# Dealing the weight preparation of a DLRM tower anew over the prologue and steps 0 to 6

## The reference, cut to what matters

```
e  = stack of 26 table rows per sample            # 512 x 26 x 64, gathered by ids
x  = layer_norm(dense @ Wd.T, gd, bd)             # 512 x 128
y  = layer_norm(e @ Ws.T, gs, bs)                 # 512 x 26 x 128
y  = layer_norm(y^T @ Wsi, gsi, bsi)^T            # 512 x 32 x 128
T  = concat(x, y)                                 # 33 vectors of 128 per sample
Z  = lower triangle of T T^T                      # 528 products per sample
z  = layer_norm(Z @ Wl.T, gl, bl)[:384]
h  = relu(concat(z, dense) @ W_top1 + b_top1)     # 512
h  = relu(h @ W_top2 + b_top2)                    # 256
out = h @ W_top3
```

## Time and profile before

| | us |
|---|---|
| median of 3 runs | 297.45 |
| lowest, highest | 296.03, 299.9 |
| span of the profiled execution, first to last instruction | 185.4 |
| the rest of the median, outside the span | 112.05 |
| PE / DVE / ACT / POOL busy | 148.0 / 130.1 / 106.9 / 104.3 |
| mean granted clock of TensorE | 0.936 |

### The profile page before, as it was taken

One profiled execution on the slowest core, in us unless ns is written; L12 is line 12 of the kernel. 1 busy time (PEld: TensorE's weight loads), 2 busy tenths in 40 slices (PEclk: granted clock), 3 DMA queues, 4 the chain that ended last, 5 costly groups with the idle time before them and its releaser, 6 DMA issues.

```text
span 185.4 us, 4668 instructions
## 1 busy us (share of the span) xinstructions
PE 148.0 (80%) x1825; PEld 113.2 (61%) x1825; DVE 130.1 (70%) x300; ACT 106.9 (58%) x245; POOL 104.3 (56%) x111
## 2 busy tenths in 40 slices
PE   0089877977969947459996978899799799977995
PEld 0084544434549544419794947569596666877994
DVE  6269659772959594908697999579799967943142
ACT  1202435594868486866667877585877857831230
POOL 3778777877878777777777777777840000020000
PEclk9999999996999669855999999999999999997899
DMA  5816334141111112311111123111111100110000
GB/s 153 294 33 194 137 58 161 32 139 26 34 21 29 24 28 61 61 27 27 28 33 23 32 58 64 28 28 25 28 25 40 33 7 11 27 38 0 0 0 0
DMA packets 6003, 9.59 MB, mean 52 GB/s; under 512 B 2303, under 2 KB 3538, under 8 KB 5854
## 3 DMA queue, kind: packets, MB, share of 16 engines
q0 software_dynamic: 3392, 3.45, 10.3%
q1 hardware_dynamic: 2232, 5.08, 9.1%
q10 hardware_dynamic: 358, 0.78, 1.1%
HBM read 8.01 MB, written 0.00 MB: 43 GB/s over the span
## 4 chain that ended last, share of the span: by engine, by line
PE 40%; ACT 23%; DVE 19%; issue 11%; DMA 5%; ACTq 1%; DVEq 0%
PE psB L318 11%; ACT Zs L639 10%; DVE B L831 4%; ACT U L600 4%; DMA dense_sb<-in_dense 4%; PE psG L284 4%; DVE qA L809 4%; DVE prod L802 3%; PE psZ L333 3%; PE psW L352 3%; PE psU L299 3%; DVE ssB L838 3%; ACT sdB L617 2%; PE psB L520 2%; PE psZ L424 2%
## 5 line engine op out<-in xcount | busy, mean ns | idle before, releaser
L257 POOL DMA_INDIRECT g_sb<-in_table,row_id x104 | 102.8, 989 | 31.7 <-issue 31.4
L831 DVE TENSOR_TENSOR B<-psB,bias 128x512 f32<-128x512 f32 x31 | 20.0, 686 | 26.2 <-PE psB L318 26.2
L639 ACT ACTIVATE Zs<-psZ 32x264 f32<-32x264 f32 x59 | 36.3, 616 | 2.1 <-PE psZ L333 1.0
L318 PE MATMUL psB<-U,ws_g 64*128 64x512 f32 x64 | 20.9, 735 | 15.3 <-ACT U L600 15.2
L611 ACT ACTIVATE sqB<-B 128x512 f32<-128x512 f32 x31 | 19.1, 632 | 23.1 <-DVE B L831 23.1
L299 PE MATMUL psU<-wsi_x,g_sb 128*128 128x192 f32 (+4 forms) x128 | 23.3, 330 | 7.3 <-DVE g_sb L824 7.3
L299 PEld LDWEIGHTS psU<-wsi_x,g_sb 128*128 128x128 f32 x128 | 20.9, 206 | 11.1 <-DVE g_sb L824 11.0
L284 PEld LDWEIGHTS psG<-gram,sT 128*128 128x128 f32 x104 | 14.0, 207 | 14.5 <-ACT sT L587 10.0
L850 DVE TENSOR_TENSOR T<-B,rB 128x512 f32<-128x512 f32 x31 | 21.5, 692 | 1.1
L838 DVE TENSOR_REDUCE ssB<-sqB 128x16 f32<-128x512 f32 x32 | 21.7, 677 | 0.1
L284 PE MATMUL psG<-gram,sT 128*128 128x128 f32 x104 | 17.2, 308 | 0.7 <-ACT sT L587 0.7
(11 more groups left out here) (159 smaller groups left out, 226.7 us busy)
## 6 DMA issues: line engine op xcount, KB each, us to landing
g_sb<-in_table,row_id POOLq DMA_INDIRECT x104, 2.5
wl_sb<-in_wl SPq DMA_DIRECT2D x1, 1280.0 KB, 6.0
w_sb<-in_w SPq DMA_DIRECT2D x2, 512.0 KB, 5.4
w_sb<-in_w SPq DMA_DIRECT2D x1, 768.0 KB, 4.5
small_sb<-in_small SPq DMA_DIRECT2D x1, 615.5 KB, 4.1
dense_sb<-in_dense ACTq DMA_DIRECT2D x1, 512.0 KB, 7.3
Zt<-Zs SPq DMA_DIRECT2D x3, 80.0 KB
Zt<-Zs SPq DMA_DIRECT2D x3, 70.0 KB
```

The source lines that it names most:

```text
L257: pool.indirect_dma_start(g_sb[:, k, h * DSP:(h + 1) * DSP], None, table, bass.IndirectOffsetOnAxis(row_id[:, 2 * k + h:2 * k + h + 1], 0) ...
L318: pe.matmul(psB[h][:, :], ws_g[h * DSP:(h + 1) * DSP, :], U[h * DSP:(h + 1) * DSP, u % 2, :], start=not (last and h == 0), stop=True).then ...
L639: act.activation(to, product, ACT.Copy).then_inc(Z_kept, 1)
L831: dve.tensor_tensor(B[:, h, :].rearrange("p (s j) -> p s j", j=PROJ), psB[h][:, :].rearrange("p (s j) -> p s j", j=PROJ), bias[:, :].rearr ...
```

## The change

It moves work and two orders; what is computed stays. The parts:

1. `am`, `dj` and `gg` are made by VectorE ahead of `wsi_c`, `ws_g` after nine `spread`s; the two gain and shift passes over `xn` come after `scale_a(0)`; `wl_off` is made at the end of the prologue, not in step 3.
2. `wl` is loaded when `dense` has landed, not after the 8th gather.
3. ScalarE sums the five `wl` pieces in the prologue (before: steps 1 and 2), scales them in steps 0, 1, 2 (before: 4 and 5), and takes the shift row in step 2 (before: 5).
4. `hd` is no longer made in the prologue and step 0 and biased in place in steps 5 to 8; it leaves PSUM with its bias in steps 4 (two), 5 and 6, from `dense_part` in steps 3 (two), 4 and 5. `linear(0)` and `variance(0)` now wait for it.
5. The x transposes go to psZ and stand in step 0 between `transposes(1)` and `project(0)`; `shift_part` moves to the prologue and step 0, `bias_part` to step 2, `b1_z` to step 3, `w1_g` from steps 4 to 6 to steps 2 to 4, the statistics of the shift row from step 3 to step 1.
6. `deviation_w` and `relu2` go behind `keep_u` and `rows_out`; `recip_w` goes to the end of its VectorE step.
7. In each step ScalarE's preparation stands behind `rows_out`, ahead of `squares_b`, not at the step's end.

```diff
@@ sync queue
-            sp.wait_ge(gathered[3], 32)
+            sp.wait_ge(d_dense, 16)
             sp.dma_start(wl_sb[:, :, :], wl).then_inc(d_wl, 16)
@@ TensorE
             def project(u):
...
-                    pe.wait_ge(xT_ready, 1)
+                    pe.wait_ge(x_stat, 4)
...
             def linear(b, lo, hi):
...
                         pe.wait_ge(m_kept, 1)
+                        pe.wait_ge(hd_ready, K1 - 1)
...
             def variance(b):
...
-                    pe.wait_ge(bz_ready, 1)
+                    pe.wait_ge(hd_ready, K1)
...
             def dense_part(f):
                 if f == 0:
                     pe.wait_ge(d_w1d, 16)
-                if f >= 2:
+                    pe.wait_ge(m_kept, 1)
+                elif f == 1:
+                    pe.wait_ge(bz_ready, 1)
+                else:
                     pe.wait_ge(hd_ready, f - 1)
...
-            dense_part(0)
-            dense_part(1)
...
             norms(0)
-            x_part()
-            dense_part(2)
+            shift_part(0, 2)
...
+                if t == 0:
+                    x_part()
                 project(t)
...
                 if t == 0:
-                    dense_part(3)
+                    shift_part(2, CW)
                 if t == 1:
                     x_sum()
-                    shift_part(0, 2)
                 if t == 2:
-                    shift_part(2, CW)
+                    bias_part()
                 if t == 3:
-                    bias_part()
+                    dense_part(0)
+                    dense_part(1)
+                if t == 4:
+                    dense_part(2)
+                if t == 5:
+                    dense_part(3)
@@ ScalarE
             def keep_hd(f):
                 act.wait_ge(hd_done, f + 1)
-                act.activation(hd[:, f, :], psD[f][:, :], ACT.Copy).then_inc(hd_ready, 1)
+                act.activation(hd[:, f, :], psD[f][:, :], ACT.Identity, bias=b1_z[:, f:f + 1]).then_inc(hd_ready, 1)
...
+            def prepare(t):
+                if t == 0:
+                    act.wait_ge(x_tr, 1)
+                    act.activation(xT[:, :], psZ[:, :], ACT.Copy).then_inc(xT_ready, 1)
+                    act.wait_ge(w_prep, 7)
+                    scale_wl(0)
+                    scale_wl(1)
+                if t == 1:
+                    scale_wl(2)
+                    scale_wl(3)
+                if t == 2:
+                    keep_x()
+                    scale_wl(4)
+                    keep_m()
+                if t == 4:
+                    act.wait_ge(bz_ready, 1)
+                    keep_hd(0)
+                    keep_hd(1)
+                if t == 5:
+                    keep_hd(2)
+                if t == 6:
+                    keep_hd(3)
...
             rows_out(0)
+            act.wait_ge(d_wl, 16)
+            for jj in range(CW - 1):
+                sum_wl(jj)
             deviation_a(0)
-            keep_hd(2)
+            sum_wl(CW - 1)
...
-                if late and j == 0 and b:
-                    relu2(b - 1)
-                if late and j == 2:
-                    deviation_w(b)
                 keep_u(t)
                 if t + 1 < UNITS:
                     rows_out(t + 1)
                 else:
                     third_squares(0)
+                if late and j == 0 and b:
+                    relu2(b - 1)
+                if late and j == 2:
+                    deviation_w(b)
+                prepare(t)
...
-                if 5 <= t < 5 + K1:
-                    f = t - 5
...
-                    act.activation(hd[:, f, :], hd[:, f, :], ACT.Identity, bias=b1_z[:, f:f + 1]).then_inc(hd_biased, 1)
@@ VectorE
-                if late and j == 2:
-                    recip_w(b)
...
-                if t == 3:
+                if t == 1:
                     dve.wait_ge(m_done, 1)
...
-                if t == 4:
+                if t == 3:
                     dve.wait_ge(bz_done, 1)
...
+                if late and j == 2:
+                    recip_w(b)
+                if 2 <= t < 2 + KZ:
+                    k = t - 2
```

More of the change, by code:

```diff
@@ L690, in keep_hd, with sum_wl, scale_wl @@
                 act.wait_ge(hd_done, f + 1)
[L691 to L694 removed]
+                act.activation(hd[:, f, :], psD[f][:, :], ACT.Identity, bias=b1_z[:, f:f + 1]).then_inc(hd_ready, 1)
+            def sum_wl(jj):
+                act.activation(wl_g[:, jj, :], wl_sb[:, jj, :], ACT.Identity,
+                               accum_out=wl_sum[:, jj:jj + 1]).then_inc(wl_summed, 1)
+            def scale_wl(jj):
+                act.activation(wl_g[:, jj, :], wl_sb[:, jj, :], ACT.Identity, bias=wl_off[:, jj:jj + 1],
+                               scale=gg[:, jj:jj + 1]).then_inc(wl_scaled, 1)
@@ new lines, in keep_x, with keep_m @@
+            def keep_x():
+                act.wait_ge(x1_done, 1)
+                act.wait_ge(fills, 5)
+                act.activation(Zt[EXTRA:EXTRA + 2, :, :, 0, :],
+                               psH[EXTRA:EXTRA + 2, :].rearrange("p (b h s) -> p b h s", b=BLOCKS, h=2),
+                               ACT.Identity, bias=one_row[EXTRA:EXTRA + 2, :]).then_inc(x1_ready, 1)
+            def keep_m():
+                act.wait_ge(m_shift, 1)
+                act.wait_ge(wl_scaled, CW)
+                act.activation(wl_g[0:NA, 0, :], psW[0:NA, :], ACT.Identity, bias=m_off[0:NA, :],
+                               scale=g_i[0:NA, :]).then_inc(m_kept, 1)
@@ L954, in _ @@
             dve.tensor_reduce(wsi_sum[:, :], wsi, AX, ALU.add).then_inc(w_prep, 1)
-            dve.wait_ge(d_rows, 16)
-            dve.wait_ge(w_prep, 3)
-            dve.tensor_tensor(ws_g[:, :], ws_c[:, :], gs_b, ALU.mult).then_inc(w_prep, 1)
+            one_j3 = one_j.rearrange("p (c j) -> p c j", c=CW)
+            dve.tensor_scalar(dj[:, :, :], one_j3, b_i, None, ALU.mult)
+            dve.tensor_scalar(am[:, :, PROJ], at_x, b_i, None, ALU.mult)
+            dve.tensor_scalar(am[:, :, PROJ + 1], b_j, b_i, float(E), ALU.mult, ALU.mult)
+            dve.tensor_scalar(gg[:, :], g_j, g_i, None, ALU.mult).then_inc(w_prep, 1)
+            dve.wait_ge(w_prep, 4)
+            for jj in range(CW):
+                last = dve.scalar_tensor_tensor(out=am[:, jj, 0:PROJ], in0=one_i, scalar=b_j[:, jj:jj + 1],
+                                                in1=dj[:, jj, :], op0=ALU.mult, op1=ALU.add)
+            last.then_inc(am_ready, 1)
             dve.scalar_tensor_tensor(
@@ L993, in _ @@
             last.then_inc(x_stat, 1)
+            dve.wait_ge(bias_done, 1)
+            dve.tensor_copy(bias[:, :], psU[:, 0:PROJ]).then_inc(bias_kept, 1)
+            mult_a(0)
+            sums_a(0)
+            recip_a(0)
+            scale_a(0)
             dve.wait_ge(x_stat, 4)
@@ L999, in _ @@
                               bd_b.rearrange("p (o e) -> p o e", o=1).broadcast_to([P, 4, E]), ALU.add).then_inc(x_col, 1)
-            dve.wait_ge(bias_done, 1)
-            dve.tensor_copy(bias[:, :], psU[:, 0:PROJ]).then_inc(bias_kept, 1)
-            mult_a(0)
-            sums_a(0)
-            recip_a(0)
-            scale_a(0)
-            one_j3 = one_j.rearrange("p (c j) -> p c j", c=CW)
-            dve.tensor_scalar(dj[:, :, :], one_j3, b_i, None, ALU.mult)
-            dve.tensor_scalar(am[:, :, PROJ], at_x, b_i, None, ALU.mult)
-            dve.tensor_scalar(am[:, :, PROJ + 1], b_j, b_i, float(E), ALU.mult, ALU.mult)
-            dve.tensor_scalar(gg[:, :], g_j, g_i, None, ALU.mult).then_inc(w_prep, 1)
-            dve.wait_ge(w_prep, 6)
-            for jj in range(CW):
-                last = dve.scalar_tensor_tensor(out=am[:, jj, 0:PROJ], in0=one_i, scalar=b_j[:, jj:jj + 1],
-                                                in1=dj[:, jj, :], op0=ALU.mult, op1=ALU.add)
-            last.then_inc(am_ready, 1)
+            dve.wait_ge(wl_summed, CW)
+            dve.scalar_tensor_tensor(out=wl_off[:, :], in0=wl_sum[:, :], scalar=-1.0 / FLIN, in1=gg[:, :],
+                                     op0=ALU.mult, op1=ALU.mult).then_inc(w_prep, 1)
             def step(t):
```

47 lines of the change are left out of this document (7 added, 40 removed).

## The result

| | us |
|---|---|
| before, median of its runs beside these | 298.67 |
| changed kernel, median of 4 runs | 287.25 (286.18 to 291.6) |
| ratio, with its 95% interval | 0.9617 [0.9528, 0.9706] |
| forecast | 290.65, range 289.0 to 295.2 |
| span of the changed kernel's profiled execution, and that execution's own time | 284.4, 286.18 |

The change makes the kernel 3.8% faster, by 11.4 us. The forecast had the direction, and 6.8 us. Some runs of every kernel are a few per cent slower than its others; the medians hold all runs, the ratios leave the slow ones out.

A forecast was written before the change was run, and what follows sets the result against it. A loop over TensorE, ScalarE and VectorE was taken to bound the kernel, with gathers as ceiling. 6.95 + 0.25 = 7.2 us, less 0.4 for the clock, is 6.8: span 178.6 plus 112.05 gives 290.65, range 289.0 to 295.2.

The forecast's parts named there:

- The ceiling: At units 4 to 12, gather landings limit the gain: unit 4 at most 2.4 us earlier, unit 12 at most 6.95.
- the forecast's own signs of being wrong: Wrong if unit 8 starts over 1 us behind its gather, half clock exceeds two steps behind 46, or gathers move.
- The 112 us around the span: Time outside the profiled span of 185.4 us, taken as the same 112.05 us before and after the change.
- Steps 3 to 6: Unit 4 to unit 8: 30.0 + 0.4 + 1.4 us from 48.6 gives 80.4, then 2.5 of wait for the gather.
- the evictions with bias: On ScalarE in its wait for add_b: each between 0.60 and 0.68 us; two in step 4 are free.
- Step 7: An in-place bias (0.68) and the root (0.37) leave ScalarE's list ahead of keep_u(8): with overlap 0.8 us saved.
- steps 8 to 14: recip_w on VectorE at keep_u(9) costs 0.66 us, relu at keep_u(10) saves 0.5, unit 12 to the end saves 0.25.
- Steps 0 to 2: TensorE is ready for unit 4 well before 48.6, then idles about 2.5 us until its gather lands.
- the price of a half clock: At project(7), behind a 2.5 us wait: between 0 and 1.5 us, less 0.6 of slack; 0.4 taken.
- A: Clock rival: new waits at units 4 and 8 put three steps at half clock, 3.35 us lost, 293.6; chance 0.22.
- C: Slower: gather waits in steps 3 to 14 drop the clock, 2.15 us a step, 313 with all twelve; chance 0.05.
- B: Waits change places in steps 3 to 6; only the 2.4 us up to unit 4 come through, 295.05; chance 0.14.

The follow-up runs named there:

- e1: The kernel before, unedited, run once more for its profile: 299.85 us, ratio 0.9987, span 297.4.
- e4: Changed kernel with only block 0 gathered by GpSimd (26 of 104 gathers), other blocks' rows read by plain loads: 192.69 us.
- e5: Kernel before with only block 0 gathered by GpSimd, other blocks' rows read by plain loads: 202.89 us.
- e15: Kernel before, with GpSimd clearing a 128x512 scratch tile behind each gather as a pause: 231.1 us, ratio to before 0.7776.
- e16: Changed kernel, with GpSimd clearing a 128x512 scratch tile behind each gather as a pause: 233.02 us, ratio 0.7805.
- e2: Kernel before with only the new orders of relu2, deviation_w and recip_w: 301.71 us against 301.76 of before beside it.
- e3: Changed kernel with the old orders of relu2, deviation_w and recip_w: 290.05 us, ratio 0.9676.

## Why the prediction was wrong

*The ceiling (the step that failed).* "However much work leaves the loop, unit 4 can start 2.4 us earlier and unit 12 6.95 us earlier, no more, as long as the gathers keep their pace." It took the gathers' landings as the bound of a steady pace. In the executions that are timed, the engines stand until about 16 us behind the issue of the last gather (after: 132.9 to 148.9), and keep_u(3), at 161.7, comes 29 us behind that issue. Unit 8 starts at 191.6, not near 82.9, which was one of the forecast's own signs of being wrong. From there nothing is bounded by gathers, and work taken out of the loop comes through whole. e1 shows it in the kernel before, e4 and e5 show that the standing goes with the gathers, and e15 with e16 that a ceiling does hold once the engines are freed: there the change is worth nothing that can be told.

*The 112 us around the span (the cause of that).* The prediction said "both sides carry the same 112.05". Of 297.45 us a good 110 were a wait in the span that its one profiled execution did not have. In number this is the larger part of the miss: the two sides did not carry the same remainder, since the wait's end, read at keep_u(2), came 3.4 us earlier in after than in e1. Why that one execution was spared is open; no other profile here looks like it. It was not the gathers' distance, for GpSimd issued them 1.25 us apart there as well:

```profile
61.18 0.94 POOL L257 DMA_INDIRECT g_sb<-in_table,row_id  x1 [0.30 <-issue]
62.43 0.94 POOL L257 DMA_INDIRECT g_sb<-in_table,row_id  x1 [0.30 <-issue]
```

*Steps 3 to 6.* Forecast 7.5 a step at full clock, 31.8 for four with the four-chunk unit and the dense pair. Measured 8.3 + 7.3 + 7.3 + 7.4 = 30.3. Before took 8.7 + 9.4 + 10.3 + 9.2 = 37.6. The 7.3 us between them are the gain that the ceiling should have cut to (89.8 - 51.0) - (82.9 - 48.6) = 4.5. A plain step took 7.3 where 7.5 was taken, and the dense pair with the four-chunk unit cost 1.0 where 1.4 + 0.4 was; the evictions with bias took 0.69 and 0.70, the upper of the two bounds, and were covered.

*Step 7 and steps 8 to 14.* Forecast -0.8 for step 7, measured 9.4 to 8.7. Forecast for the seven steps behind it +0.66 - 0.5 - 0.25 = -0.1, measured +0.2; e2, where the orders stand alone, gives +0.2 too. Right to within 0.3 us. (Of the -0.25, 0.4 rest on a wait for gathers at unit 12, which did not exist; without them the sum is +0.3.)

*Steps 0 to 2.* That "whatever is wrong so far, by up to 2 us, vanishes in the wait there" was true in a way not meant: these steps crawl through the long wait. The start of step 2 moved by 3.4 us between e1 and after; e2 has it at 159.8 and e3 at 155.8, so that much also comes and goes with where the crawl ends.

*The sum.* The forecast's own engine terms, left without the ceiling, are 38.8 - 31.8 = 7.0 for steps 3 to 6, 0.8 for step 7 and 0.1 behind it, 7.9 us; measured behind keep_u(2) are 8.1 (0.3 + 8.0 - 0.2). The ceiling and the price of a half clock cut this to 6.8. So the ceiling was wrong in kind, but took only about 1 us from the number. The rest of the 13.0 is the start, 3.4, and the tail, 1.5; the tail is chance, and that the change moves the start is not shown. So some 8 us of the 11.4 are traced to the change, and the rest is not accounted for.

*The rivals.* A and C put the clock at half behind waits for gathers. The low clock in steps 5 and 6 was before's, behind waits for the other engines, and the change removed it. In after the clock is 0.55 through the long wait and at full from 170 on, in a part where no gather is waited for, so neither could come. The Trainium skill ("TensorE: Matmul & The Clock Gate", section "HAM oscillation") says that bursts with waits between them start cold each time; the stretch 21 to 149 with its 0.55 agrees, and the steps behind it, whose waits are fractions of a microsecond, show the other side. B, that the waits change places and the gain stops, did not happen in the kernel as it is; e15 and e16 come nearest to its case.

## What to carry to other kernels

Hold the span of a profile against the measured time before any working: if over a hundred microseconds are left, as here, the profile may be of another case than the runs, and neither its ceilings nor its waits may be used for them until a second profile has settled it. Where a queue is fed without a pause, try it with small pauses before tuning the engines around it; here pauses took the changed kernel from 287.25 to 223.63, the whole change gave 11. And put an engine's preparation in the wait that its step has anyway, early enough for the work of another engine that waits for it in the same step.

## What the runs showed of the hardware

- While GpSimd issues indirect gathers 1.25 us apart, the other engines hardly move in all executions but one: VectorE idles for up to 42.6 us at a time in e1, although each instruction lasts as long as ever. It begins near 17 to 30 us and ends behind the last gather: in e4 that gather is issued at 35.0 and TensorE goes on at 41.5, in after at 132.9 and 148.9. The one execution that was spared, the first profile of before, had the same distance between gathers, so the distance alone does not bring the wait about. At 1.55 us apart TensorE's gaps are 3.8 us at most.
- Matmuls too are held one by one where no wait of the program stands between them. TensorE in e1, inside inner(0):

```profile
117.27 0.55 PE L333 MATMUL psZ<-T 128*32 128x33 f32 x22
120.03 0.21 PE L333 MATMUL psZ<-T 128*32 128x33 f32 x1 [2.21 <-issue]
122.13 0.22 PE L333 MATMUL psZ<-T 128*32 128x33 f32 x1 [1.88 <-issue]
126.33 0.21 PE L333 MATMUL psZ<-T 128*32 128x33 f32 x1 [3.98 <-issue]
```

and in after, as the hold ends:

```profile
148.17 0.21 PE L334 MATMUL psZ<-T 128*32 128x33 f32 x1 [0.49 <-issue]
148.88 0.71 PE L334 MATMUL psZ<-T 128*32 128x33 f32 x32 [0.50 <-issue]
```

So the 64 matmuls of inner(0) do not come in one run. The starts of the single ones lie 2.10 and 4.20 us apart, and 0.71 at the end of the hold: multiples of 0.70 us. Once it ends, 32 matmuls take 0.71 us together.
- One reading is a backlog: something that serves a gather takes about 1.4 us, twice these 0.70, and other work stands in line behind it. In after TensorE goes on at 148.9, and (148.9 - 3) / 104 = 1.40 us a gather; between 1.34 and 1.55 us the hold fades. That is an inference; no run looked at the thing itself, and it does not say why the first profile of before was spared. Signals between the engines cannot be all that stands in line, since the matmuls above wait for none.
- A rival that no run tests is that the recording of the execution takes a part in the hold. The traces of e1 and after hold 669 and 660 of the semaphore events of transfers, the first profile of before 2094. So "issue" and "remote" in these traces can be waits whose event is missing.
